# Two of eight groups of conditioning matrices fetched by plain transfers from two more queues, beside the gather

## What is computed

```python
w = weights[conditions]                        # (32, 32, 32) out of (200, 32, 32)
y = jnp.einsum('bct,bcd->bdt', x, w)           # x is (32, 32, 256)
h = silu(einsum('bsh,hi->bsi', y, w_gate)) * einsum('bsh,hi->bsi', y, w_up)   # 256 -> 1024
h = sparsify_2to4(h)                           # of each 4 neighbours the 2 largest |h| stay
out = x + einsum('bsi,ih->bsh', h, w_down)     # 1024 -> 256
```

## Time and profile before

| what | before |
|---|---|
| time, median of 3 runs | 80.88 us (80.46 to 80.88) |
| the profiled execution's own time | 80.44 us |
| its span, first to last instruction | 78.6 us |
| TensorE busy with matmuls | 74.5 us, 95% |
| VectorE busy | 62.1 us, 79% |
| ScalarE busy | 41.7 us, 53% |
| GpSimd busy | 8.6 us, 11% |

### The profile page before, as it was taken

One profiled execution on the slowest core, in us unless ns is written; L12 is line 12 of the kernel. 1 busy time (PEld: TensorE's weight loads), 2 busy tenths in 40 slices (PEclk: granted clock), 3 DMA queues, 4 the chain that ended last, 5 costly groups with the idle time before them and its releaser, 6 DMA issues.

```text
span 78.6 us, 1020 instructions
## 1 busy us (share of the span) xinstructions
PE 74.5 (95%) x362; PEld 59.5 (76%) x362; DVE 62.1 (79%) x91; ACT 41.7 (53%) x61; POOL 8.6 (11%) x18
## 2 busy tenths in 40 slices
PE   3999999999999999999999999999999999999950
PEld 1338778888888888888888888888888888888840
DVE  0017691699879999599999979999999999994460
ACT  6122753869453375599897769789380402730000
POOL 5550000000000013000713000006200000000000
PEclk9999999999999999999999999999999999999999
DMA  0857559984900004900099990003995000003333
GB/s 1 250 183 201 232 154 381 413 377 92 425 33 0 0 0 79 188 0 0 15 194 200 194 198 13 4 0 60 200 177 96 0 0 0 8 0 138 137 142 118
DMA packets 3221, 9.64 MB, mean 123 GB/s; under 512 B 496, under 2 KB 752, under 8 KB 2960
## 3 DMA queue, kind: packets, MB, share of 16 engines
q0 software_dynamic: 928, 3.28, 21.9%
q1 hardware_dynamic: 2144, 6.16, 21.8%
q10 hardware_dynamic: 144, 0.13, 0.5%
HBM read 5.38 MB, written 1.05 MB: 82 GB/s over the span
## 4 chain that ended last, share of the span: by engine, by line
PE 95%; POOL 1%; DVE 1%; issue 0%; POOLq 0%
PE banks L558 52%; PE banks L600 28%; PE banks L520 6%; PE banks L543 4%; PE banks L570 4%; PE banks L529 1%; POOL warm L199 1%; DVE gate_raw L435 1%; POOLq L663 0%
## 5 line engine op out<-in xcount | busy, mean ns | idle before, releaser
L558 PE MATMUL banks<-y_hl,up_hl 128*128 128x512 f32 x96 | 24.2, 389 | 0.0
L600 PE MATMUL banks<-h_hl,down_hl 128*128 128x512 f32 (+1 forms) x102 | 22.0, 376 | 0.0
L558 PE MATMUL banks<-y_hl,gate_hl 128*128 128x512 f32 x84 | 21.4, 390 | 0.0
L600 PEld LDWEIGHTS banks<-h_hl,down_hl 128*128 128x128 f32 x102 | 18.5, 188 | 3.6
L558 PEld LDWEIGHTS banks<-y_hl,up_hl 128*128 128x128 f32 x96 | 18.0, 188 | 3.8
L558 PEld LDWEIGHTS banks<-y_hl,gate_hl 128*128 128x128 f32 x84 | 15.7, 188 | 3.2
L243 ACT ACTIVATE silu<-banks 128x512 f32<-128x512 f32 x16 | 9.6, 597 | 12.4 <-PE banks L558 12.1
L384 DVE TENSOR_TENSOR h<-banks,silu 128x512 f32<-128x512 f32 x12 | 8.3, 689 | 4.4 <-ACT silu L243 4.4
L264 ACT ACTIVATE h_hl<-h 128x1024 fp32r<-128x1024 f32 (+1 forms) x8 | 6.7, 843 | 3.9 <-DVE h L420 3.9
L420 DVE SCALAR_TENSOR_TENSOR h<-count,h 128x512 f32<-128x512 bf16 x12 | 7.9, 687 | 0.1
L520 PE MATMUL banks<-warm 128*128 128x512 bf16 x12 | 4.8, 586 | 1.3 <-POOL warm L199 1.3
(11 more groups left out here) (39 smaller groups left out, 68.1 us busy)
## 6 DMA issues: line engine op xcount, KB each, us to landing
h_hl<-h POOLq DMA_DIRECT2D x4, 512.0 KB, 6.1
x_sb<-in_x SPq DMA_DIRECT2D x2, 512.0 KB, 3.4
up_raw<-in_w_up SPq DMA_DIRECT2D x2, 512.0 KB, 4.7
down_raw<-in_w_down SPq DMA_DIRECT2D x1, 1024.0 KB, 7.8
gate_raw<-in_x_t SPq DMA_DIRECT2D x1, 1024.0 KB, 4.8
down_hl<-down_raw POOLq DMA_DIRECT2D x2, 512.0 KB, 5.0
out<-gate_raw SPq DMA_DIRECT2D x3, 256.0 KB, 2.4
gate_raw<-in_w_gate SPq DMA_DIRECT2D x2, 256.0 KB, 3.3
```

The costliest lines, as they stand in the source:

```text
L558: last = nc.tensor.matmul(dst, w_hl[w][:, s, q, k, j], y_hl[:, m, half, k], start=i == 0, stop=i == len(terms) - 1)
L600: last = nc.tensor.matmul(bank[:, begin:end], down_hl[:, s, q, j, k * P:(k + 1) * P], h_hl[:, u, m, j, begin:end], start=(q, j, m, s) == f ...
```

## The change

The matrices of groups 0 and 1 no longer come from the gather. ScalarE and SP each read four table indices into registers and issue four transfers of one 32x32 matrix, straight to the place where the transpose would have put it. The gather still brings eight groups: its order is rolled by two, so that its first half holds groups 2 to 5 and its second 6, 7 and again 0 and 1 (unused). `x`'s first half is issued by GpSimd, and the memset for the zero matmuls is done by VectorE; there are 8 of these matmuls instead of 12. The gate and up weights of the first `q` come in two halves of the columns, so that the first transfers are half as large. The mixing goes group by group. The last two output transfers change their issuing engines.

```diff
-    WARM_START = 12
+    WARM_START = 8
@@ sync
             sp.dma_start(cond_sb[:], cond).then_inc(cond_in, 16)
-            sp.dma_start(x_sb[:, 0:GH, :], x[0]).then_inc(x_in[0], 16)
-            sp.dma_start(raw_w[0][:, 0, 0], w_gate[0, 0]).then_inc(first_in[0], 16)
+            _, chosen = nc.values_load_multi_w_load_instructions(
+                cond_list[:, NB:2 * NB], engines=(mybir.EngineType.SP,),
+                skip_runtime_bounds_check_because="the transfers check their own bounds")
+            for b in range(NB):
+                sp.dma_start(mix_w[b * C:(b + 1) * C, 1, 0],
+                             matrices[bass.ds(chosen[b], 1)].rearrange("o c d -> (o c) d")).then_inc(early_in[1], 16)
+            sp.dma_start(raw_w[0][:, 0, 0, 0:2 * P], w_gate[0, 0, 0]).then_inc(first_in[0], 16)
 
             sp.wait_ge(mix_in[0], 16)
@@ gpsimd
-            nc.gpsimd.memset(warm[:], 0.0).then_inc(warm_zero, 1)
+            pool.dma_start(x_sb[:, 0:GH, :], x[0]).then_inc(x_in[0], 16)
@@ scalar
+            _, chosen = nc.values_load_multi_w_load_instructions(
+                cond_list[:, 0:NB], engines=(mybir.EngineType.Activation,),
+                skip_runtime_bounds_check_because="the transfers check their own bounds")
+            for b in range(NB):
+                act.dma_start(mix_w[b * C:(b + 1) * C, 0, 0],
+                              matrices[bass.ds(chosen[b], 1)].rearrange("o c d -> (o c) d")).then_inc(early_in[0], 16)
             act.wait_ge(warm_zero, 1)
@@ vector
+            nc.vector.memset(warm[:], 0.0).then_inc(warm_zero, 1)
             dve.wait_ge(cond_in, 16)
+            dve.wait_ge(blocks_marked, 1 + NB)
             nc.vector.tensor_tensor(rows_sb[:], cond_sb[:, 0:NH], cond_sb[:, NH:2 * NH], ALU.add).then_inc(rows_done, 1)
-            dve.wait_ge(blocks_marked, 1 + NB)
-            transpose_rows(0)
             diagonal(SPANS[0])
             diagonal(SPANS[1])
+            transpose_rows(0)
+            diagonal(SPANS[2])
@@ tensor
+            def first_mixing():
+                mixing_by_batch(0)
+                mixing(0, 1)
+                mixing_by_batch(1)
+                mixing(1, 1)
+                for g in range(EARLY, GH):
+                    last = mixing_by_batch(g)
                 last.then_inc(mixed, 1)
...
+                for g in range(EARLY, GH):
+                    last = mixing(g, 1)
+                last.then_inc(mixed, 1)
@@
             warm_up(WARM_START)
-            pe.wait_ge(w_hi, pieces_until(0, 0, 0))
-            mixing_by_batch()
-            mixing(0, 1)
+            pe.wait_ge(w_hi, pieces_until(0, 0, 0, 0))
+            first_mixing()
             first_gates()
```

More of the change, by code:

```diff
@@ L99, in adaln_ffn @@
         transposed = sem("transposed")
+        early_in = [sem(f"early_in{g}") for g in range(EARLY)]
         diag_done = sem("diag_done")
@@ L142, in adaln_ffn @@
         Y_PIECES = [(0, k, k + 1) for k in range(KT)] + [(1, 0, KT)]
[L145 to L153, removed]
+        SPANS = [slice(0, 1), slice(1, EARLY), slice(EARLY, GH), slice(GH, NG)]
+        GATE_PIECES_END = PIECES.index((1, 0, 0, KT, 0, M)) + 1
         OUTPUTS = [(0, 0, 0, TH, y_banks[:, 0]), (0, 1, 0, TH, y_banks[:, 1]),
@@ L189, in _ @@
             sp.dma_start(xt_sb, x_t).then_inc(xt_in, 16)
-            for i, (half, k, begin, end, _) in enumerate(OUTPUTS[:-1]):
-                if i != UNFINISHED:
+            for i, (half, k, begin, end, _) in enumerate(OUTPUTS):
+                if i not in (UNFINISHED, LEFT):
                     cols = slice(half * TH + begin, half * TH + end)
@@ L354, in diagonal @@
             def diagonal(groups):
-                half, shape = groups.start // GH, [P, groups.stop - groups.start, NB, D]
-                dve.wait_ge(transposed, half + 1)
+                shape = [P, groups.stop - groups.start, NB, D]
+                if groups.stop > EARLY:
+                    dve.wait_ge(transposed, 1 if groups.stop <= GH else NH)
+                for g in range(groups.start, min(groups.stop, EARLY)):
+                    dve.wait_ge(early_in[g], 16 * NB)
                 mark = own_block.rearrange("p (o b z) -> p o b z", o=1, z=1)
@@ L446, in _ @@
                 low_y(k)
-            for i in range(KT, 2 * KT):
+            for i in range(KT, LATER):
                 low_weights(i)
@@ L520, in warm_up @@
                     nc.tensor.matmul(gate_bank(0), warm[:, 0:P], warm[:], start=True, stop=True)
[L522 to L530, removed]
-                last.then_inc(mixed, 1)
@@ L533, in mixing, with mixing_by_batch @@
[L533 to L546, removed]
+            def mixing_by_batch(g):
+                if g < EARLY:
+                    pe.wait_ge(early_in[g], 16 * NB)
+                else:
+                    pe.wait_ge(transposed, 1)
+                if g == 0:
+                    pe.wait_ge(x_in[0], 16)
+                for b in range(NB):
+                    rows = slice(b * C, (b + 1) * C)
+                    last = nc.tensor.matmul(banks[:, b, g * D:(g + 1) * D], x_sb[rows, g, 0:P],
+                                            mix_w[rows, g, 0], start=True, stop=True)
+                return last
@@ L547, in mixing, with second_mixing @@
+            def second_mixing():
+                pe.wait_ge(x_in[1], 16)
+                pe.wait_ge(y_lo, KT)
+                for k in range(KT):
+                    for g in range(GH, NG):
+                        last = mixing(g, k)
                     last.then_inc(mixed, 1)
@@ L552, in split_product @@
                 for i, (s, m, k) in enumerate(terms):
-                    if half == 0 and j == 0:
-                        pe.wait_ge(w_hi if s == HI else w_lo, pieces_until(q, w, k))
+                    if half == 0 and (j == 0 or (q, j) == (0, 2)):
+                        pe.wait_ge(w_hi if s == HI else w_lo, pieces_until(q, w, k, j))
                     if q == 0 and j == 0:
@@ L656 @@
         "cond": cond,
-        "table": table,
-        "w_gate": columns(inputs["L0_ffn_w_gate"]).transpose(0, 2, 1, 3),
+        "cond_list": _np.asarray(inputs["itok_B_1_198"]).reshape(1, B),
+        "table": chunks,
+        "matrices": table,
+        "w_gate": columns(inputs["L0_ffn_w_gate"]),
         "w_up": columns(inputs["L0_ffn_w_up"]),
```

104 lines of the change are left out of this document (68 added, 36 removed).

## The result

The changed kernel takes 86.3 us (85.39 to 86.78, 6 runs) where the kernel before, in the same number of runs beside it, takes 80.75: a ratio of 1.0641, with an interval of 1.0577 to 1.0705. The time lies outside the range given. The ratios here leave out executions that were over 1.5% above the fastest of the same kernel, though where an experiment is on TensorE's clock these are part of what it measures, so that its times are given with them. With all six against all six the ratio of the medians is 1.069.

What follows compares the result with a forecast made beforehand. It took TensorE's unbroken chain (95% busy) as the bound, movable by when real work begins, the clock's pace or a new hole. 80.44 + 0.86 for the later start + 0.18 for y's copy = 81.5 us; range 79.8 to 82.9.

Steps and rivals of the forecast that it cites:

- The sign: Whole kernel: slower, 81.5 us against a profiled 80.44; chance 0.44 of slower than within 0.5%.
- Which piece decides: Head of the timeline: the first gate piece, behind SP's loads and four issues, sets when the mixing starts.
- The terms of the start: SP's path: loads 1.3, four issues 1.84, landing 2.2, copy 0.42 us; TensorE starts at 7.1, 0.86 later.
- The 2.6 us: SP's register loads: the alternative total at 1.3 us a load, which would put the sum 1.3 higher.
- Work at the high clock: Mixing and first gates on TensorE: clock high or nearly so after the hole, nothing added to the sum.
- the clock rival: TensorE after the hole: clock still low, mixing and first gates slower by at most 2.2 us; chance 0.16.
- My bound: Mixing and first gates: clock low until as much work again (4.5 us) is done, at most 2.2 us more.
- 3.4 us of work may do: Zero matmuls: the argument against a low clock, that eight of them, 3.4 us, may suffice to raise it.
- rival 3: TensorE's clock low after the hole: 82.2 to 83.7 us, first gates 0.43 apart, not 0.24; chance 0.16.
- The cover of y's copy: Between mixing and first gates: two block matmuls instead of four hide less of y's high copy, 0.18 us.
- Rival 1: Head of the timeline: loads and issues are cheap, mixing starts at 5.4, 79.6 to 80.4 us; chance 0.32.
- Its threshold: SP's path: TensorE starts before 6.24 when loads, four issues and landing together take under 4.35 us.

Runs made afterwards that it cites:

- a_warm20: The changed kernel with 20 zero matmuls instead of 8; 83.44 us, ratio 1.0337.
- b_warm8: The kernel before with 8 zero matmuls instead of 12, nothing else changed; 82.3 us, ratio 1.0185.
- a_no_early: The changed kernel without early matrices: the gather brings all groups, old mixing order, 12 zero matmuls; 80.87 us, ratio 1.0053.
- a_late_whi: The changed kernel with 12 zero matmuls and the wait for w_hi moved from the first mixing matmul to the first gates; 81.37 us, ratio 1.0103.
- a_gate_first: The changed kernel with SP's first gate piece issued ahead of the register loads, and 12 zero matmuls; 83.27 us.
- a_fixed: The changed kernel with groups 0 and 1 from fixed table places, no indices read, 12 zero matmuls; 82.05, 83.28, 83.35 and 84.72 us.
- a_warm12: The changed kernel with 12 zero matmuls instead of 8; 85.4 us, ratio 1.0595.

## Why the prediction was wrong

The sign was right and the size was not: 81.5 was forecast, 86.3 measured, outside the 79.8 to 82.9. The step that failed is the one on TensorE's clock, which the sum held high at no cost; it cost 2.70 us.

**Which piece decides.** Right. The first mixing matmul waits for ScalarE's copy of the gate piece (7.24 to 7.67), behind SP's loads and issues.

**The terms of the start.** The two loads were taken at 1.3 us and took 1.50; the four issues at 1.84 and took 2.13; the landing at 2.2 and took 2.38; the copy at 0.42 and took 0.43. The start came at 7.71 instead of 7.1, so that this term was 1.47 instead of 0.86. The loads are also not of one length: the indices took 0.49, 0.92 and 1.29 us in three executions of a changed kernel. The Trainium skill's about 200 ns for a register (Runtime: NRT & Kernel Launch, "Instruction fetch mechanics") gives an estimated 1.2 us for six. This trace has 1.36 for the two instructions, near it in the sum alone: the load of the address, two registers by the prediction's count, took 0.87, and that of four indices 0.49. The 2.6 us that the prediction worked out from 1.3 us for each load is not borne out.

**Work at the high clock.** This is the step that failed. The forecast kept the clock high, at no cost, and gave the clock rival 0.16 with at most 2.2 us; by the traces of the changed kernel and of a_warm20 it cost 2.70 (8.63 - 5.93). b_warm8 shows the loss in the kernel before alone (1.7 us for four zero matmuls fewer), and a_warm20 that filling the hole takes 2.9 us off the changed kernel although its start was later. My bound took the clock as low until as much work had been done as before its rise (4.5 us). In the profiled execution it was high when the mixing began and fell 0.5 us into it, and stayed low for 6.8 us of unbroken work. "3.4 us of work may do" was half true there: the clock did rise (the first records are fast), but did not stay. The first gates stood 0.34 us apart on average (4.12 / 12), between rival 3's 0.43 and the 0.24 of before, because the clock rose again in their midst.

**The cover of y's copy, 0.18 us.** The term itself was right (0.14 by a_warm20), but a second one was missing: I costed the group-by-group order only by what it no longer hides, and put the alternation at nothing without a reason. At the high clock the mixing takes 2.91 us in the new order and 2.11 in the old, 0.8 us, of which 0.67 is the alternation.

**Rival 1, faster from 5.4 us.** Excluded. Its mechanism fails at a place that I had not priced: the small transfers share the transfer engines with `x`, so that even with no loads and issues ending at 2.58 the matrices were usable at 5.95. Its threshold had a slip: by the prediction's own terms the three may take 6.24 - 1.19 - 0.57 = 4.48 us and not 4.35, which changes nothing in the verdict, since they took 6.0.

**The sum by the runs**: 1.47 for the start, 0.84 for mixing and gates at the high clock (5.93 in a_warm20 against 5.09 before, 0.73 of it in the mixing), and 2.70 for the clock make 5.01, for an execution that was 5.08 slower. The median was 5.55 over the kernel before; the last half microsecond, with the four executions from 86.18 to 86.78, stays open.

## What to carry to other kernels

Zero matmuls ahead of the first real work are part of the schedule: if the work starts later, or one cannot tell when, they must reach up to it; four too few cost 1.7 us in the kernel before, more than the late gate piece cost in the changed one (1.47). Before a gather is replaced by direct transfers, add up the register loads, the issues one behind the other and what already fills the transfer engines, and look at everything that stands behind the new instructions in the same queue; here the direct way brought one group of four matrices at 6.2 us where the gather had four groups at 6.1. And a new order of small matmuls is to be priced as work, not only by what it uncovers.

## What the hardware showed unexpectedly

The clock's fall came after the work had begun again, not in the hole: 0.5 us into the mixing in the changed kernel, and 1.9 us into it in b_warm8, near 8.3 us, nearly all of its mixing being at full pace.

The length of the hole alone does not tell whether the clock is kept. With 12 zero matmuls each and a hole of 0.73 us in the traced execution, a_no_early kept it in four of four executions; a_late_whi with 0.69 in three of four; a_gate_first, whose only hole of note was 0.40 behind group 0's small matmuls, in one of four; a_fixed with 1.28 in one of four; a_warm12 with 1.11 in none of five. (Kept: a mean granted clock of at least 0.99. The holes differ between executions, and only one of each was traced.) What decides in the cases between was not shown.

With 10 zero matmuls in the kernel before, the same program took between 80.33 and 83.73 us. Transfers of 4 KB issued by 2.6 us were usable at 5.95 us with 512 KB under way from another queue, and at 3.85 without it.
